# Expert tiles of 128 tokens regrouped as 16 pairs and 7 singles, with weights fetched per slot

## The chip, the core and the metric

The kernel runs on one core of a Trainium2 chip. TensorE (PE) multiplies, VectorE (DVE) and ScalarE (ACT) work element by element and read what PE wrote to PSUM, GpSimd (POOL) here does some elementwise work and issues the indexed transfers (gathers and scatters), and SyncE (SP) issues plain transfers. Each engine takes its instructions in the order of the program and waits on semaphores. The metric is the device time of one execution in microseconds.

## The reference

The input is 8 sequences of 256 tokens with 128 features. After a layer norm, two branches are added to it: a retention layer of 16 heads, and a mixture of 8 experts of which every token takes two:

```
scores = einsum('bnd,ed->bne', xn, expert_tokens)
_, topk_idx = top_k(scores, 2)
for i in range(8):
    w = mean(topk_idx == i, axis=-1)            # 0 or 0.5
    h = gelu(xn @ W1[i] + b1[i])                # 128 -> 512
    h = gelu(h @ W2[i] + b2[i])                 # 512 -> 512
    outputs += (h @ W3[i] + b3[i]) * w          # 512 -> 128
```

Everything is float32. The biases are not zero.

## The kernel before, in words

First comes the retention stage: eight batches `b` of 256 tokens in a hand-written order on each engine. During batches 0 to 5, DVE also works out the routing in small chained instructions (`step`, counted by the semaphore `v_disp`; the constants `D_...` say after which count a result is there): for each of 4096 token-expert assignments a slot in a list, sorted by expert and padded to tiles of 128. The lists `gidx` and `sidx` hold for every tile the tokens to gather and to scatter to. `expert_of_tile` writes the expert of each tile to `exi`. Normed tokens lie in device memory as `xnd`.

The expert stage is a loop over 39 tiles of 128 tokens. For a tile, POOL gathers the rows (`gather`, into one of four `xg`), PE transposes them (`trans_x`), ACT copies them to `xf`, PE does the first layer, DVE adds the bias, ACT applies Gelu (`gelu1`), ACT and DVE split the result into a high and a low part (`h1h`, `h1l`). The second layer is 12 float32r matmuls with 512 moving columns: the hidden state is stationary and the weights move, high and low parts of both. DVE adds the bias, ACT applies Gelu, PE transposes four blocks (`trans2`), ACT copies, PE does the third layer, DVE scales and adds the bias (`out3`, into one of two `ys`), and POOL adds the rows to the output in device memory (`scatter`).

All weights of all eight experts lie in SBUF. Those of the second layer are loaded in 32 pieces of 128 x 512 and split into `w2h` and `w2l` beside the retention stage, the last twelve after it (`w2_high`, `w2_low`, `w2_both`). The matmuls pick the expert by a register. First-layer weights are copied to `w1c` by DVE for each tile (`fetch`).

PE's order per tile is second layer of t, input transpose of t+3, third layer of t-1, first layer of t+2, `trans2` of t. POOL's order is gather of t+4, then scatter of t-1; each scatter waits until the one before has landed, since both add to the same rows.

Of the kernel before, what the change touches and what calls it, by code (L numbers as in the profile page):

```python
# [15 lines left out]
NT = 39  # L16
NTP = 40
LATE = 3
# [9 lines left out]
C_REP = 1661  # L28
C_N = 2173
# [5 lines left out]
def constants():  # L35
# [17 lines left out]
    c[:, C_IT:C_IT + NTP] = np.arange(NTP)  # L53
    c[:, C_K:C_K + 16] = 128 * np.arange(16)
# [15 lines left out]
def moe_retention_kernel(nc, x, wqkv, wvo, gb, etokT, w1, w2, w3, b1t, b23, cf, cb, out):  # L70
# [4 lines left out]
    R0 = 16512  # L75
    W2H, W2L = R0, R0 + 65536
    W1O, W3O = R0 + 131072, R0 + 147456
    B2O, B3O = R0 + 163840, R0 + 180224
    F0 = R0 + 184320
    w2h = at("w2h", 8 * 2048, F32R, W2H)  # L80
    w2l = at("w2l", 8 * 2048, F32R, W2L)
    w1s = at("w1s", 8 * 512, F32, W1O)
    w3s = at("w3s", 8 * 512, F32, W3O)
    b2s = at("b2s", 8 * 512, F32, B2O)
    b3s = at("b3s", 8 * 128, F32, B3O)
    o = F0
    ident = at("ident", 128, F32, o); o += 512
    gidx = at("gidx", NTP, U32, o); o += 160
    sidx = at("sidx", NTP, U32, o); o += 160
    ex = at("ex", NTP, F32, o); o += 160  # L90
    exi = at("exi", NTP, I32, o); o += 160
    b1s = at("b1s", 32, F32, o); o += 128
    stg = [at(f"stg{i}", 512, F32, o + 2048 * i) for i in range(4)]; o += 8192
    G0 = o


    xg = [at(f"xg{i}", 128, F32, o + p) for i, p in enumerate((1536, 512, 1024, 0))]; o += 2048
    xf = [at(f"xf{i}", 128, F32, o + 512 * i) for i in range(2)]; o += 1024
    w1c = at("w1c", 512, F32, o); o += 2048
    g1 = at("g1", 512, F32, o); o += 2048  # L100
    h1h = at("h1h", 512, F32R, o); o += 2048
    h1l = at("h1l", 512, F32R, o); o += 2048
    g2 = at("g2", 512, F32, o); o += 2048
    h2t = [at(f"h2t{i}", 512, F32, o + 2048 * i) for i in range(2)]; o += 4096
    ys = [at(f"ys{i}", 128, F32, o + 512 * i) for i in range(2)]; o += 1024
    assert o <= 229368


    o = G0
    cs = at("cs", 384, F32, o); o += 1536  # L110
    small = at("small", C_REP - C_P, F32, o); o += 512
    cbs = at("cbs", B_N, BF16, o); o += 896
    wq = at("wq", 512, F32, o); o += 2048
    et = at("et", 8, F32, o); o += 32
    mv = at("mv", 32, F32, o); o += 128
    st = at("st", 96, F32, o); o += 384
    vs = at("vs", 128, F32, o); o += 512
    qr = [at("qr0", 256, F32, o), at("qr1", 256, F32, o + 1024)]; o += 2048
    kr = [at("kr0", 256, F32, o), at("kr1", 256, F32, o + 1024)]; o += 2048
    qh = at("qh", 256, F32R, o); o += 1024  # L120
    rstd = at("rstd", 16, F32, o); o += 64
    o += 32
    wv = at("wv", 256, F32, o); o += 1024
    gbt = at("gbt", 2, F32, o); o += 32
    xr = [at(f"xr{i}", 256, F32, o + 1024 * i) for i in range(2)]; o += 2048
    rt = at("rt", 256, F32, o); o += 1024
    sq = at("sq", 256, F32, o); o += 1024
    rn = at("rn", 256, F32, o); o += 1024
    ob = at("ob", 256, F32, o); o += 1024
    vr = at("vr", 32, F32, o); o += 128  # L130
    eps = at("eps", 1, F32, o); o += 32
    nb = at("nb", 16, F32, o); o += 64
    assert o <= 229368, o
    A0 = W2H + 40960
    B0 = W2L + 40960
    C0, D0, E0 = W3O + 10240, B2O, W1O + 10240

    o = A0
    oh = [at(f"oh{i}", 128, BF16, o + 256 * i) for i in range(8)]; o += 2048
    bt = at("bt", 16 * NTP, BF16, o); o += 1280  # L140

    s1 = at("s1", 128, F32, A0)
    cm = at("cm", 128, F32, A0 + 512)
    past = at("past", 7 * NTP, F32, A0)
    sc = at("sc", 128, F32, A0 + 1024)
    s0 = at("s0", 128, F32, A0 + 1536)
# [97 lines left out]
    def sync():  # L244
# [17 lines left out]
        for i in range(4):  # L262
            load_w2(i)
# [1058 lines left out]
```

## Time and profile before

| | |
|---|---|
| median of 3 runs | 378.18 us (377.08 to 378.86) |
| profiled execution, own time | 378.94 us |
| its span, first to last instruction | 377.2 us |
| mean granted TensorE clock | 0.953 |
| PE busy | 315.3 us, 84% |
| DVE, ACT, POOL busy | 238.7, 183.3, 181.3 us |
| HBM read, written | 21.61 MB, 4.65 MB |

The retention stage takes the first 150 us or so, then 14 us pass until the second layer of the first tile starts at 164.22, and the tiles run until the end. Busy time of PE counts overlapping matmuls once; a matmul's own duration holds its depth, so that the step from one start to the next says more.

### The profile page before, as it was taken

How to read it: one execution, taken by the hardware profiler on the slowest of the kernel's cores; microseconds unless marked ns; L12 is line 12 of the kernel's file. 1: busy time of each engine (PE TensorE's matmuls, PEld its weight loads, DVE VectorE, ACT ScalarE, POOL GpSimd, SP SyncE). 2: the span in 40 equal slices, each digit the busy share in tenths (PEclk: the TensorE clock that was granted, in tenths of full speed). 3: DMA queues.
4: the chain of work that ended last, by engine and by line, in shares of the span. 5: the costliest groups of instructions: out<-in, count | busy, mean ns of one | idle time of the engine just before them, and what ended most of it. 6: DMA issues, size and time to landing. Idle time of an engine off the chain costs nothing.

```text
span 377.2 us, 7594 instructions
## 1 busy us (share of the span) xinstructions
PE 315.3 (84%) x2304; PEld 269.6 (71%) x2304; DVE 238.7 (63%) x471; ACT 183.3 (49%) x390; POOL 181.3 (48%) x169
## 2 busy tenths in 40 slices
PE   0995958777686897459999999999999999999960
PEld 0793846656484675348888988898888889888850
DVE  5659899899989887744555454455545455555410
ACT  4463355466554675624554454455455445445420
POOL 8106256465655443752444455544455554444331
PEclk9999699899988999869999999999999999999995
DMA  8270292122231238801112221111221111222000
GB/s 260 93 223 30 76 323 78 56 58 56 57 106 40 89 108 330 295 22 16 22 28 28 29 30 19 29 24 24 30 28 27 23 21 27 30 24 24 5 2 0
DMA packets 25109, 26.31 MB, mean 70 GB/s; under 512 B 3712, under 2 KB 18048, under 8 KB 24944
## 3 DMA queue, kind: packets, MB, share of 16 engines
q1 hardware_dynamic: 14080, 13.69, 11.8%
q0 software_dynamic: 6864, 4.67, 9.1%
q10 hardware_dynamic: 4128, 7.47, 5.7%
q8 instruction: 22, 0.36, 0.4%
q14 instruction: 15, 0.12, 0.1%
HBM read 21.61 MB, written 4.65 MB: 70 GB/s over the span
## 4 chain that ended last, share of the span: by engine, by line
PE 68%; DVE 15%; issue 8%; ACT 3%; DMA 2%; POOL 1%; ACTq 0%; DVEq 0%; SPq 0%; POOLq 0%
PE ps L194 60%; PE ps L1186 5%; DVE qx L696 3%; DVE pt L703 2%; DVE tmp L672 2%; DVE w2l L737 1%; DMA xn<-in_x 1%; PE ps L1147 1%; PE ps L988 1%; DVE bt L613 1%; PE ps L994 1%; DVE kr L677 1%; DVE vr L716 1%; DVE bt L610 1%; DMA out<-ys,sidx 1%
## 5 line engine op out<-in xcount | busy, mean ns | idle before, releaser
L919 POOL DMA_INDIRECT out<-ys,sidx x39 | 62.0, 1589 | 95.0 <-DVE ys L775 90.4
L767 DVE TENSOR_TENSOR g<-ps,b2s 128x512 f32<-128x512 f32 x39 | 27.0, 691 | 79.9 <-PE ps L194 79.9
L194 PE MATMUL ps<-w2l,h1h 128*128 x156 | 65.4, 419 | 4.6 <-DVE w2l L737 4.6
L194 PE MATMUL ps<-w2h,h1h 128*128 x156 | 61.7, 396 | 0.0
L194 PE MATMUL ps<-w2h,h1l 128*128 x156 | 61.3, 393 | 0.0
L403 ACT CAST h1h<-g 128x512 fp32r<-128x512 f32 x39 | 24.1, 619 | 56.0 <-PE ps L194 55.9
L912 POOL DMA_INDIRECT xg<-xnd,gidx x39 | 39.1, 1004 | 15.7 <-issue 10.6
L397 ACT ACTIVATE g<-g 128x512 f32<-128x512 f32 x39 | 24.7, 634 | 42.6 <-DVE g L751 42.6
L888 POOL TENSOR_SCALAR_AFFINE_SELECT pt<-pt 128x512 f32<-128x512 f32 x24 | 16.3, 677 | 57.5 <-ACT pt L294 57.5
L194 PE MATMUL ps<-xf,w1c 128*128 128x128 f32 x312 | 41.4, 276 | 2.6 <-ACT xf L393 2.0
L194 PE MATMUL ps<-w3s,h2t 128*128 x312 | 41.2, 275 | 0.8 <-ACT h2t L413 0.8
L194 PEld LDWEIGHTS ps<-w3s,h2t 128*128 128x128 f32 x312 | 38.0, 191 | 4.4 <-issue 1.0
L194 PEld LDWEIGHTS ps<-xf,w1c 128*128 128x128 f32 x312 | 38.0, 192 | 3.2 <-issue 3.1
L194 PEld LDWEIGHTS ps<-w2l,h1h 128*128 128x128 f32 x156 | 29.8, 191 | 9.8 <-issue 4.9
L751 DVE TENSOR_TENSOR g<-ps,b1s 128x512 f32<-128x512 f32 x39 | 27.0, 691 | 15.1 <-PE ps L194 14.4
L194 PEld LDWEIGHTS ps<-w2h,h1h 128*128 128x128 f32 x156 | 29.6, 190 | 7.0
L194 PE MATMUL ps<-qx,kst 128*128 128x512 f32 x64 | 31.8, 501 | 2.9 <-DVE pt L703 1.5
L194 PEld LDWEIGHTS ps<-w2h,h1l 128*128 128x128 f32 x156 | 29.9, 192 | 5.1
L407 ACT ACTIVATE g<-g 128x512 f32<-128x512 f32 x39 | 24.6, 630 | 8.0 <-DVE g L767 3.2
L761 DVE TENSOR_TENSOR h1l<-g,h1h 128x512 fp32r<-128x512 f32 x39 | 28.0, 719 | 0.6 <-ACT h1h L403 0.6
L703 DVE TENSOR_TENSOR pt<-ps,cs 128x512 f32<-128x512 f32 x40 | 27.0, 680 | 1.3 <-PE ps L194 1.1
L696 DVE CAST qx<-ps 32x512 fp32r<-32x512 f32 x32 | 22.2, 693 | 6.2 <-PE ps L194 5.7
(137 smaller groups left out, 599.6 us busy)
## 6 DMA issues: line engine op xcount, KB each, us to landing
stg<-in_w SPq DMA_DIRECT2D x24, 256.0 KB, 2.7
b2s<-in_b ACTq DMA_DIRECT2D x1, 2048.0 KB, 10.4
w2l<-in_w SPq DMA_DIRECT2D x4, 512.0 KB, 5.9
w1s<-in_w ACTq DMA_DIRECT2D x1, 1280.0 KB, 7.5
xn<-in_x SPq DMA_DIRECT2D x4, 256.0 KB, 4.7
xnd<-xn SPq DMA_DIRECT2D x1, 1024.0 KB, 6.1
xr<-in_x SPq DMA_DIRECT2D x8, 128.0 KB, 3.4
out<-ob SPq DMA_DIRECT2D x8, 128.0 KB, 3.2
```

The source lines that it names most:

```text
L194: mm = lambda o_, l, r, s=True, p=True: T.matmul(o_, l, r, start=s, stop=p, skip_group_check=True)
L397: A.activation(g1[:], g1[:], ACT.Gelu).then_inc(a_g1, 1)
L403: A.copy(h1h[:], g1[:]).then_inc(a_h1h, 1)
L407: A.activation(g2[:], g2[:], ACT.Gelu).then_inc(a_g2, 1)
L696: e = V.tensor_copy(qv[rows, :, i, m, :], r3(ps[(0, 5)[i]][rows, :], 2, 256))
L703: V.tensor_tensor(r3(pt[n % 6][:], 4, 128), r3(ps[3 + n % 2][:], 4, 128), cmask.unsqueeze(1).to_broadcast([128, 4, 128]), ALU.mult).then_i ...
L751: V.tensor_tensor(r3(g1[:], 4, 128), r3(ps[0][:], 4, 128), b1s[:, bass.ds(vregs[t] * 4, 4)].unsqueeze(2).to_broadcast([128, 4, 128]), ALU. ...
L761: V.tensor_tensor(h1l[:], g1[:], h1h[:], ALU.subtract).then_inc(v_h1l, 1)
L767: V.tensor_tensor(g2[:], ps[2][:], b2s[:, bass.ds(vregs[t] * 512, 512)], ALU.add).then_inc(v_b2, 1)
L912: G.indirect_dma_start(xg[t % 4][:], None, xnd, bass.IndirectOffsetOnAxis(ap=gidx[:, t:t + 1], axis=0)).then_inc(d_g[t % 4], 16)
L919: G.indirect_dma_start(out, bass.IndirectOffsetOnAxis(ap=sidx[:, t:t + 1], axis=0), ys[t % 2][:], None, bounds_check=NTOK - 1, oob_is_err= ...
L1186: e = T.transpose(ps[3][:, 128 * c:128 * c + 128], g2[:, 128 * c:128 * c + 128], ident[:])
```

## The change

The 39 tiles become 23 slots: 16 pairs of two tiles of the same expert and then 7 single tiles (`SLOTS`). The routing gives each expert its full pairs in the first 32 tile numbers and its odd tile in the last seven, with 18 more chained instructions.

For a pair, the moving operand is 256 tokens wide. In the second layer the weights are now stationary and the hidden state moves, so that the result comes out transposed already: 48 matmuls of 256 columns for two tiles, no `trans2`, and bias and Gelu in one ACT instruction per 256 columns, read from PSUM. Singles keep the form of before, but their bias comes after the transposes.

Weights are fetched per slot by SP: `wa` (first- and third-layer weights and biases, 128 x 1160, four buffers) and `raw` (second layer, 128 x 2048, three buffers). ACT casts the whole 128 x 2048 to `w2h`, DVE subtracts to `w2l` in place; for the first three slots POOL does the latter, beside the retention stage. There are four `ys` instead of two, and the scatter stands three tiles behind the loop's tile.

```
+NPAIR, NONE = 16, 7
+SLOTS = [(2 * i, 2 * i + 1) for i in range(NPAIR)] + [(2 * NPAIR + j,) for j in range(NONE)]
...
-    D_GT, D_MSK, D_POS, D_IDX, D_EXP, D_ALL = 5, 7, 13, 24, 27, 33
+    D_MSK, D_POS, D_EXP, D_ALL = 7, 23, 45, 51
...
+        def load_weights(i, which):
+            t = last(i)
+            e = nc.sync.value_load(exi[0:1, t:t + 1], min_val=0, max_val=NEXP - 1)
+            if which != "w2":
+                if i >= 4:
+                    P.wait_ge(v_ys, last(i - 4) + 1)
+                P.dma_start(was[i % 4][:], wa[bass.ds(e, 1)]...).then_inc(d_wa[i % 4], 16)
+            if which != "wa":
+                if i >= 3:
+                    P.wait_ge(t_l2, last(i - 3) + 1)
+                P.dma_start(raw[i % 3][:], w2[bass.ds(e, 1)]...).then_inc(d_w2[i % 3], 16)
...
+        for i in range(PRE, NS):          # SP, after the retention stage; PRE = 3
+            load_weights(i, "w2")
+            if i + 1 < NS:
+                load_weights(i + 1, "wa")
...
+        for i in range(NS):               # ACT
+            if i + 1 < NS:
+                for t in SLOTS[i + 1]:
+                    gelu1(t)
+                    h1_high(t)
+            if i and wid(i - 1) == 128:
+                gelu2(last(i - 1))
+            if i + 2 < NS:
+                copy_xf(i + 2)
+                if i + 2 >= PRE:
+                    w2_high(i + 2)
+            if wid(i) == 256:
+                for t in SLOTS[i]:
+                    gelu2(t)
...
+        for i in range(NS):               # DVE
+            if i >= 2:
+                for t in SLOTS[i - 2]:
+                    out3(t)
+            if i and wid(i - 1) == 128:
+                copy_g2(last(i - 1))
+            if i + 1 < NS:
+                for t in SLOTS[i + 1]:
+                    h1_low(t)
+            if PRE <= i + 2 < NS:
+                w2_low(i + 2)
...
+        for t in range(NT):               # POOL
             if t + 4 < NT:
                 gather(t + 4)
+            if t == 3:
+                G.wait_ge(d_ob, 16 * NB)
+            if t == first(slot_of[t]):
+                half_b3(slot_of[t])
+            if t >= 3:
+                scatter(t - 3)
...
+            if wid(i) == 256:             # layer2, PE
+                for k in range(2):
+                    out_ = bank[:, 256 * k:256 * k + 256]
+                    for c in range(4):
+                        ...
+                        mm(out_, wl[:, w], hi[:, cc], c == 0, False)
+                        mm(out_, wh[:, w], lo[:, cc], False, False)
+                        e = mm(out_, wh[:, w], hi[:, cc], False, c == 3)
...
+        for i in range(NS):               # PE
+            if i + 1 < NS:
+                for t in SLOTS[i + 1]:
+                    layer1(t)
+            if i and wid(i - 1) == 128:
+                trans2(last(i - 1))
+            if i + 2 < NS:
+                for t in SLOTS[i + 2]:
+                    trans_x(t)
+            for t in SLOTS[i]:
+                layer2(t)
+            if i:
+                for t in SLOTS[i - 1]:
+                    layer3(t)
```

One turn of the loops over slots is called turn i below.

POOL's order in the expert stage, before: a gather (L912) and a scatter (L919) in turn. The first row gathers tile 6, the second scatters tile 1, the third gathers tile 7; `d_g`, `t_gT`, `d_s` and `v_ys` are the semaphores of gathers landed, input transposes done, scatters landed and `ys` written.

```order
L912 DMA xg2_67<-xnd,gidx_56 128x128 [waits t_gT]
L919 DMA out_0<-ys1_79,sidx_57 2048x128 [waits d_s,v_ys]
L912 DMA xg3_68<-xnd,gidx_56 128x128 [waits t_gT]
L919 DMA out_0<-ys0_78,sidx_57 2048x128 [waits d_s,v_ys]
L912 DMA xg0_65<-xnd,gidx_56 128x128 [waits t_gT]
```

The same place now, with tiles 0, 8, 1, 9 and 2 in the DMA rows (L903 scatters, L896 gathers, L883 halves a slot's third-layer bias):

```order
L903 DMA out_0<-ys0_76,sidx_82 2048x128 [waits v_ys,d_ob]
L896 DMA xg0_62<-xnd,gidx_81 128x128 [waits t_gT]
L883 TENSOR_SCALAR wa2_60<-wa2_60 128x128 [waits d_wa2]
L903 DMA out_0<-ys1_77,sidx_82 2048x128 [waits d_s,v_ys]
L896 DMA xg1_63<-xnd,gidx_81 128x128 [waits t_gT]
L903 DMA out_0<-ys2_78,sidx_82 2048x128 [waits d_s,v_ys]
```

The gather of tile t+4 stood behind the scatter of tile t-2, six tiles back, and stands now behind that of tile t-4, eight tiles back.

PE's order around one tile before, from the end of one second layer to the start of the next (L1147 is the input transpose, L1186 `trans2`, L194 a matmul):

```order
L194 MATMUL ps2<-w2h_49,h1h_73 128x512
L1147 MATMUL ps5<-ident_55,xg1_66 128x128 [waits a_xf,d_g1]
L194 ISA [waits v_ys,a_h2]
L194 MATMUL ps4<-w3s_52,h2t1_77 128x128
...
L194 MATMUL ps0<-xf0_69,w1c_71 128x128 [waits v_w1c,v_b1,a_xf]
L194 MATMUL ps0<-xf0_69,w1c_71 128x128 x3
L1186 MATMUL ps3<-ident_55,g2_75 128x128 [waits a_h2,a_g2]
L1186 MATMUL ps3<-ident_55,g2_75 128x128 x3
L194 ISA [waits v_b2,v_h1l]
L194 MATMUL ps2<-w2l_50,h1h_73 128x512
```

PE now, from the end of one pair's third layer (L150 is a matmul, L1129 the input transpose):

```order
L150 MATMUL ps5<-wa3_61,h21_74 128x128 x3
L150 MATMUL ps2<-xf0_66,wa2_60 128x256 [waits a_g1,d_wa2,a_xf]
L150 MATMUL ps2<-xf0_66,wa2_60 128x256
L150 MATMUL ps0<-xf0_66,wa2_60 128x256 [waits a_h2,d_wa2,a_xf]
L150 MATMUL ps0<-xf0_66,wa2_60 128x256
L1129 MATMUL ps5<-ident_80,xg2_64 128x128 [waits v_ys,a_xf,d_g2]
L1129 MATMUL ps5<-ident_80,xg3_65 128x128 [waits v_ys,a_xf,d_g3]
L150 MATMUL ps1<-h1h1_70,w2l0_52 128x256 [waits a_h2,v_w2l,v_h1l]
```

The input transposes moved from behind a second layer to the place between the first and the second layer.

SP in the expert stage now (before, it had nothing to do there); `exi` is the list of experts, L225 loads `wa`, L229 loads `w2`:

```order
L225 ISA [waits v_ys]
L225 DMA wa2_60<-in_wa 128x1160
L221 TENSOR_LOAD exi_84
L221 ISA x2
L229 ISA [waits t_l2]
L229 DMA raw0_55<-in_w2 128x2048
```

Every load of second-layer weights is queued behind a load of `wa` that waits for `ys`.

## Rows read from the trace of the kernel before

**Rows 1.** The page: busy us, share of the span, instructions of each engine.
```profile
PE 315.3 (84%) x2304; PEld 269.6 (71%) x2304; DVE 238.7 (63%) x471; ACT 183.3 (49%) x390; POOL 181.3 (48%) x169
```

**Rows 2.** Windows: stretch, length, busy PE, PEld, DVE, ACT, POOL (instructions), clock, DMA share, GB/s.
```profile
200.00:300.00 100.00, 100.00 (x650) 89.17 (x649) 52.59 (x100) 49.47 (x99) 50.58 (x39) 1.00 0.18 26
```

**Rows 3.** The chain that ended last: start us, us, what; two of its repeating pieces.
```profile
252.51 2.76 PE ps L194 x12
255.38 1.79 PE ps L194 x16
```

**Rows 4.** Timeline of one tile's period: start us, us, engine, line, operation.
```profile
254.53 0.99 POOL L912 DMA_INDIRECT xg<-xnd,gidx  x1 [0.31 <-issue]
...
256.62 0.28 DVE L775 SCALAR_TENSOR_TENSOR ys<-ps,b3s 128x128 f32<-128x128 f32 x1
...
257.73 1.59 POOL L919 DMA_INDIRECT out<-ys,sidx  x1 [2.21 <-DVE ys L775]
...
259.62 1.00 POOL L912 DMA_INDIRECT xg<-xnd,gidx  x1 [0.30 <-issue]
```

**Rows 5.** Timeline of PE in the retention stage: matmuls with 256 moving columns.
```profile
129.67 1.03 PE L194 MATMUL ps<-xnt,wq 128*128 128x256 f32 x4
...
134.51 0.28 PE L194 MATMUL ps<-kl,repm 128*128 128x256 f32 x1
...
135.22 0.28 PE L194 MATMUL ps<-kl,repm 128*128 128x256 f32 x1
```

**Rows 6.** Timeline of PE at the start of the expert stage.
```profile
159.17 0.47 PE L1147 MATMUL ps<-ident,xg 128*128 128x128 f32 x1
164.22 0.79 PE L194 MATMUL ps<-w2l,h1h 128*128 x1 [4.58 <-DVE w2l L737]
...
168.55 0.27 PE L1147 MATMUL ps<-ident,xg 128*128 128x128 f32 x1
```

**Rows 7.** DMA issues, us to landing: from 200 to 300 us, and last from 150 to 161 us.
```profile
out<-ys,sidx POOLq DMA_INDIRECT x20, 3.2
xg<-xnd,gidx POOLq DMA_INDIRECT x19, 2.5
...
xg<-xnd,gidx POOLq DMA_INDIRECT x2, 6.6
```

**Rows 8.** DMA issues of the whole span: KB each, us to landing.
```profile
b2s<-in_b ACTq DMA_DIRECT2D x1, 2048.0 KB, 10.4
...
w1s<-in_w ACTq DMA_DIRECT2D x1, 1280.0 KB, 7.5
```

**Rows 9.** Groups by form: busy us, mean ns, idle before; elementwise instructions of several widths.
```profile
L767 DVE TENSOR_TENSOR g<-ps,b2s 128x512 f32<-128x512 f32 x39 | 27.0, 691 | 79.9 <-PE ps L194 79.9
...
L379 ACT CAST w2h<-stg 128x512 fp32r<-128x512 f32 x24 | 14.0, 618 | 0.0
...
L737 DVE TENSOR_TENSOR w2l<-stg,w2h 128x512 fp32r<-128x512 f32 x4 | 4.5, 1126 | 0.0
...
L732 DVE TENSOR_TENSOR ob<-ps,xr 128x256 f32<-128x256 f32 x8 | 3.4, 420 | 0.2
...
L300 ACT CAST kh<-kr 128x256 fp32r<-128x256 f32 x8 | 3.2, 405 | 5.3 <-DVE kr L677 5.3
...
L555 DVE TENSOR_TENSOR cm<-ne,small 128x128 f32<-128x128 f32 x1 | 0.3, 292 | 0.0
```

**Rows 10.** Timeline at the end: the last tiles' third layer, `out3` and scatters.
```profile
361.60 0.39 PE L194 MATMUL ps<-w2h,h1h 128*128 x1
...
361.82 1.05 PE L194 MATMUL ps<-w3s,h2t 128*128 x8
...
363.02 0.29 DVE L775 SCALAR_TENSOR_TENSOR ys<-ps,b3s 128x128 f32<-128x128 f32 x1 [0.22 <-PE ps L194]
...
364.09 1.55 POOL L919 DMA_INDIRECT out<-ys,sidx  x1 [3.09 <-DVE ys L775]
...
367.64 1.55 POOL L919 DMA_INDIRECT out<-ys,sidx  x1 [1.99 <-DMA out<-ys,sidx]
```

More of the change, by code:

```diff
@@ L389, in copy_xf @@
[L389 to L397 removed]
+            A.wait_ge(d_w2[i % 3], 16 * (i // 3 + 1))
+            if i >= 3:
+                A.wait_ge(t_l2, last(i - 3) + 1)
+            A.copy(w2h[i % 3][:], raw[i % 3][:]).then_inc(a_w2h, 1)
@@ new lines, in copy_xf @@
+        def copy_xf(i):
+            n = wid(i)
+            A.wait_ge(t_gT, last(i) + 1)
+            if i >= 2:
+                A.wait_ge(t_l1, last(i - 2) + 1)
+            A.copy(xf[i % 2][:, 0:n], ps[5][:, 0:n]).then_inc(a_xf, 1)
+        def gelu1(t):
+            i = slot_of[t]
+            n = wid(i)
+            bank = ps[big["l1", t] % 3]
+            A.wait_ge(t_l1, t + 1)
+            if i:
+                A.wait_ge(v_h1l, last(i - 1) + 1)
+            A.wait_ge(d_wa[i % 4], 16 * (i // 4 + 1))
+            half = t - first(i)
+            for k in range(512 // n):
+                c = 512 // n * half + k
+                e = A.activation(g1[:, n * c:n * c + n], bank[:, n * k:n * k + n], ACT.Gelu,
+                                 bias=was[i % 4][:, W_B1 + c:W_B1 + c + 1])
+            e.then_inc(a_g1, 1)
@@ L415, in scalar @@
+            half = t - first(i)
+            for k in range(512 // n):
+                c = 512 // n * half + k
+                e = A.activation(h2[i % 2][:, n * c:n * c + n], bank[:, n * k:n * k + n], ACT.Gelu,
+                                 bias=was[i % 4][:, W_B2 + c:W_B2 + c + 1])
+            e.then_inc(a_h2, 1)
         A.dma_start(small[:], cf[:, C_P:C_REP]).then_inc(d_rep, 16)
@@ L837, in vector @@
             evac(8 * b + 6)
-            if not more:
-                bias1(0)
             if b == 0:
@@ L1152, in layer1 @@
-        def layer1(t):
-            T.wait_ge(a_xf, t + 1)
-            if t:
-                T.wait_ge(v_b1, t)
-            T.wait_ge(v_w1c, t + 1)
-            if t < 2:
-                expert(t)
-            for c in range(4):
-                e = mm(ps[0][:, 128 * c:128 * c + 128], w1c[:, 128 * c:128 * c + 128], xf[t % 2][:])
+            if i:
+                T.wait_ge(a_xf, i)
+            if i >= 4:
+                T.wait_ge(v_ys, last(i - 4) + 1)
+            half = 128 * (t - first(i))
@@ new lines, in trans_x @@
+            T.transpose(ps[5][:, half:half + 128], xg[t % 4][:], ident[:]).then_inc(t_gT, 1)
+        def layer1(t):
+            i = slot_of[t]
+            n = wid(i)
+            T.wait_ge(a_xf, i + 1)
+            T.wait_ge(d_wa[i % 4], 16 * (i // 4 + 1))
+            bank = free_bank(("l1", t))
+            for k in range(512 // n):
+                c = 512 // n * (t - first(i)) + k
+                e = mm(bank[:, n * k:n * k + n], was[i % 4][:, W_1 + 128 * c:W_1 + 128 * c + 128], xf[i % 2][:, 0:n])
```

631 lines of the change are left out of this document (271 added, 360 removed).

## The prediction

> **What bounds the kernel now.** I read the busy table first, then the chain of waits, then one period of the expert stage in the timeline, and last the DMA landings. TensorE (PE) is busy 84% of the span, and between 200 and 300 us it has no idle time at all, at a granted clock of 1.00, its 2.4 GHz level [rows 1, 2]. The chain stays on PE, repeating 2.76 us (12 matmuls of the second layer) and 1.79 us (16 instructions) every 5.09 us [rows 3]: 39 tiles at PE's own pace. The reader should see that no other engine matters there. In rows 4 GpSimd (POOL) waits 2.21 us for `ys`, scatters, and issues a gather 0.30 us behind the scatter's end. That gather was for a tile three turns ahead, so the scatter in front of it cost nothing. This slack is what the change spends.
>
> **PE's work per pair.** Everything in this stage runs back to back, so the spacing counts and not the duration.
> - Second layer: 24 matmuls of 512 columns at 2.76/12 = 0.230 us [rows 3] become 48 of 256 columns. The trace has float32r matmuls of that width with a new stationary operand each time: six steps from 134.51 to 135.22 are 0.118 us each [rows 5]. 48 x 0.118 = 5.68 against 5.52 us. That the weight load could set the pace instead is excluded by the same rows.
> - First layer: four x N=256 float32 matmuls are eight instructions. Four take 1.03 us with the depth of the last one in it [rows 5]; with 0.28 for that depth, as in the rows below it, the step is at most 0.25, and two of 128 columns are 0.224. I take 0.208: 1.66 us. Before, 16 at 0.112 (1.79/16) [rows 3] = 1.79.
> - The eight transposes of the second layer's output go: -0.9 us. Third layer (1.79) and two input transposes (0.22) stay.
>
> Sum for a pair: 5.68 + 1.66 + 1.79 + 0.22 = 9.35 us against 2 x 5.09 = 10.18. If PE set the pace, 16 pairs would give 13.3 us back. The vector engine (DVE) loses its bias adds and weight copies, ScalarE (ACT) gets more small Gelus. Per pair ACT then has eight instructions of 256 columns at 0.405, two casts at 0.618, a copy of 0.4 and the cast of a slot's weights, 1.9 (below): 6.8 us; DVE 0.6 + 1.4 + 2.3 = 4.3 [rows 9]. Both fit under 9.35 and so cost nothing by themselves.
>
> **The new wait on POOL.** In turn i of the main loop PE runs first layer of slot i+1, transposes of slot i+2, second layer of slot i, third layer of slot i-1. POOL's loop is still one gather, one scatter per tile, but the scatter is now of tile t-3 and the gather of tile t+4. So the gather of tile 2i+5, which PE transposes in turn i, stands behind the scatter of tile 2i-3, and that tile's third layer is the last thing of turn i-1 (POOL's order, in the part on the change). From the end E of that third layer, by rows:
> - `out3` starts at +0.15 and ends at +0.44 (362.87 to 363.02, 0.29 long) [rows 10].
> - scatter of tile 2i-4 starts 0.83 us after its `ys` (256.90 to 257.73) [rows 4]: +1.27. It holds POOL 1.59: +2.86.
> - gather of tile 2i+4: +3.16 to +4.16.
> - scatter of tile 2i-3 waits until the other has landed: 3.2 us from issue [rows 7], +4.47, and starts 0.84 later, as 364.09 + 2.71 to 367.64 did [rows 10], 3.55 us from scatter to scatter: +5.3, to +6.9.
> - gather of tile 2i+5: +7.2, lands 2.5 us later [rows 7]: +9.7.
>
> PE has only the first layer, 1.66 us, to do meanwhile, then stands about 8 us before the second layer, which is queued behind the transposes. What follows is 0.1 + 0.22 + 5.68 + 1.79 + 0.16 (depth) = 7.95, and the loop closes: 17.65 us a pair at least, as against 10.18.
>
> Two costs come on top. First, traffic: at that moment SyncE (SP) starts loading 580 KB and 1024 KB (SP's order, same part). With the DMA engines full, gathers took 6.6 us to land instead of 2.5 [rows 7]. Bounds per loop: 0 (the weights slip between) and 4.1 + about 2 on the scatter = 6. The weights are through after some 7 us and the critical gather starts after that, so I take 1.0, near the quiet row. Second, the clock: PE was idle 4.58 us, and resumed at 164.22 at half clock (1.2 GHz); 12 matmuls took until 168.55, 4.33 us for 2.76 [rows 6]. That is +1.6. Bounds: 0 if the clock held, 7.5 if second and third layer (7.47 us) ran at the half level throughout. That row is the only restart after an idle time of this kind, so I stay near it, a little above since the gap is longer: 2.0, and 0.15 for the transposes. Pair loop: 17.65 + 1.0 + 2.15 = **20.8 us**.
>
> On the clock the Trainium skill, "TensorE: Matmul & The Clock Gate", section "HAM oscillation — how this bites in real kernels", describes a kernel whose matmul bursts are parted by DMA waits and which starts every burst cold. By that rule every one of these turns pays; with a clock that held, the pair loop would be 18.65 and the whole 26 us shorter. The trace agrees for its gap of 4.58 us. On traffic the Trainium skill, "DMA: Bandwidth & Descriptors", section "Queues, rings and completion order", says each DMA engine takes packets from its queue rows in turn, so that a gather is slowed by weights but not held until they are through. By it the 1.0 us is nearer than 6; the 6.6 us landing agrees with slowed.
>
> **The weights' own loop.** `wa` of slot j waits for `ys` of slot j-4, which `out3` writes at the start of turn j-2, and `w2` of slot j is queued behind it on SP; then ACT casts 2048 columns, DVE subtracts 2048 columns, and the next `out3` is queued behind that subtract. Loads of 1280 and 2048 KB landed after 7.5 and 10.4 us, with others beside them [rows 8]; for 1604 KB with little beside it I take 7.5 (bounds 6.5 and 9.5). Cast: 0.405 at 256 columns and 0.618 at 512 give 1.90; subtract: 0.420 and 0.691 give 2.32 (4.5 at the 1.126 of one form) [rows 9]. 7.5 + 1.9 + 2.3 + 0.3 (`out3`) + five handovers of about 0.1 = **12.5 us** a turn. It stays under 20.8 for pairs and is hidden there by PE's wait for the gather; if that wait is gone, it is what comes next (rival 1). For singles the gather is not late (eight tiles back is an old slot), so this loop sets 12.5 where the tile took 5.09.
>
> **Attention.** 18 more chained DVE instructions on counts (13 to 23, 27 to 45 in the `D_` constants), at most 0.29 each [rows 9]: up to 5.2; DVE is on the chain there, while ACT and POOL lose weight splits. I take +4 (bounds 1 and 6). The 4.58 us wait for the split weights before 164.22 goes [rows 6]; late next is the copy of slot 1's inputs behind the first Gelus, about where PE was at 159.2.
>
> **Sum against the profiled span of 377.2.** Turn 0 starts at 159.2 + 4 = 163. It has a cold first layer, 3.4, transposes 0.4, second layer about 6.2: 173. Turn 1, undisturbed: 9.35, to 182. Turns 2 to 13 have the full stall: 12 x 20.8 = 250, to 432. Turn 14 waits only for one gather (issued at +3.2, landing 4 us, then 7.95 and 2.15): 17, to 449, `ys` at 449.7. Then six turns of the weights' loop, 75: 524.7. Left are one second layer at half clock 5.1, copies and transposes 5.5, another second layer 2.8, and the 15.6 us that stood before after the last second layer began to drain (361.60 to 377.2): 29. Span 553.7. The profiled run took 1.7 us more than its span (378.94), 0.8 above the median of 378.18: **554 us**, slower by 46%.
>
> **Rivals.**
> 1. *Only the weights' loop binds.* If the gathers are somehow early, pairs run at 12.8 (two `out3`). From 182: 13 turns are 166, six more 75, tail 29.7, total 453, so 454 us. For it: the loop is there in the code in any case. Against: POOL's order.
> 2. *PE keeps the pace* (the other side). Gathers and weights stay hidden, and 9.35 holds: 377.2 - 13.3, with the saved start and the longer routing even: about 365 us, faster. It decides if the second gather lands within 1.7 us of E and the weights' loop under 9.35. Rows give 9.7 and 12.5, so little speaks for it but an ordering that I misread.
> 3. *Loaded landings.* Weights and gathers collide fully, each loop near 26: 12 x 5 more, 615 us. For it: 6.6 against 2.5. Against: the critical gather starts late in the load.
>
> **Chances.** Forecast 82%, with its own range 515 to 595 (pair loop 18.5 to 23.5, weights' loop 11.5 to 14.5, routing 1 to 6). Rival 1: 8%; rival 2: 4%; rival 3: 6%. The range 500 to 600 leaves out the rivals. A difference under 0.5% can't be told from none. Faster 0.04, same 0.01, slower 0.95.
>
> **What would show it.** PE idle before the transposes of nearly every pair, released by the gather's DMA, some 8 us; POOL's second scatter of a pair released by the first one's landing; granted clock below 1 through the pair stage, second layer at 0.118 and 0.213 us spacing; a pair period near 20.8 and a single period near 12.5 with DVE's subtract followed at once by `out3`. It would be wrong if PE's idle time ended on ACT or DVE, or if the pair period were under 15.

## The result

Measured on one chip beside the kernel before: **605.3 us** (603.5 to 606.5, 4 runs) against 378.5 us, a ratio of 1.600 with a 95% interval of 1.593 to 1.606. Forecast was 554 us: the direction and the mechanism hold, the size does not, and the time lies above the range's end of 600 us. The profiled span grew from 377.2 to 603.9 us.

### The profile page after: what moved, and what is told of

It is laid out like the page before. It is cut to its first block, busy times and chain, and to the rows that moved or that the text cites. A ratio compares the mean times of both kernels' runs of the same rounds, so it can differ in the third digit from the quotient of the medians.

```text
span 603.9 us, 7127 instructions
## 1 busy us (share of the span) xinstructions
PE 344.5 (57%) x2432; PEld 301.9 (50%) x2432; DVE 210.6 (35%) x390; ACT 210.3 (35%) x433; POOL 185.0 (31%) x178
## 3 DMA queue, kind: packets, MB, share of 16 engines
q1 hardware_dynamic: 15872, 42.54, 20.8%
## 4 chain that ended last, share of the span: by engine, by line
PE 35%; DMA 34%; DVE 11%; issue 10%; POOL 4%; ACT 3%; SPq 1%; DVEq 0%; POOLq 0%; ACTq 0%
PE ps L150 32%; DMA out<-ys,sidx 23%; DMA xg<-xnd,gidx 7%; POOL out L903 4%; DMA raw<-in_w 4%; DVE qx L706 2%; DVE pt L713 1%; DVE ys L770 1%; PE ps L1129 1%; ACT w2h L355 1%; DVE tmp L682 1%; DMA xn<-in_x 1%; PE ps L960 1%; PE ps L966 1%; DVE kr L687 1%
## 5 line engine op out<-in xcount | busy, mean ns | idle before, releaser
L903 POOL DMA_INDIRECT out<-ys,sidx x39 | 63.9, 1640 | 312.5 <-DVE ys L770 220.9
L755 DVE TENSOR_TENSOR w2l<-raw,w2h 128x2048 fp32r<-128x2048 f32 x20 | 45.9, 2293 | 227.3 <-ACT w2h L355 227.3
L1129 PE MATMUL ps<-ident,xg 128*128 128x128 f32 x39 | 16.1, 425 | 170.3 <-DMA xg<-xnd,gidx 166.1
L1129 PEld LDWEIGHTS ps<-ident,xg 128*128 128x128 f32 x39 | 6.9, 177 | 179.8 <-DMA xg<-xnd,gidx 175.1
L150 PE MATMUL ps<-h1h,w2l 128*128 128x256 f32 x256 | 85.7, 335 | 0.0
L150 PE MATMUL ps<-h1l,w2h 128*128 128x256 f32 x256 | 83.1, 325 | 0.0
L150 PE MATMUL ps<-h1h,w2h 128*128 128x256 f32 x256 | 82.6, 323 | 0.0
L150 PEld LDWEIGHTS ps<-h1h,w2l 128*128 128x128 f32 x256 | 61.1, 239 | 0.0
L150 PEld LDWEIGHTS ps<-h1l,w2h 128*128 128x128 f32 x256 | 60.4, 236 | 0.0
L150 PEld LDWEIGHTS ps<-h1h,w2h 128*128 128x128 f32 x256 | 59.9, 234 | 0.0
L355 ACT CAST w2h<-raw 128x2048 fp32r<-128x2048 f32 x23 | 43.7, 1901 | 37.9 <-DMA raw<-in_w 37.9
L896 POOL DMA_INDIRECT xg<-xnd,gidx x39 | 41.9, 1074 | 11.2 <-issue 10.9
L150 PE MATMUL ps<-wa,h 128*128 128x128 f32 x312 | 39.7, 280 | 1.2 <-ACT h L401 1.2
L150 PEld LDWEIGHTS ps<-wa,h 128*128 128x128 f32 x312 | 38.4, 196 | 2.2 <-ACT h L401 1.5
L150 PE MATMUL ps<-xf,wa 128*128 128x256 f32 (+1 forms) x184 | 38.8, 355 | 0.0
L150 PE MATMUL ps<-qx,kst 128*128 128x512 f32 x64 | 30.9, 487 | 3.6 <-DVE pt L713 1.6
```

Source lines behind the costliest of these rows:

```text
L150: mm = lambda o_, l, r, s=True, p=True: T.matmul(o_, l, r, start=s, stop=p, skip_group_check=True)
L355: A.copy(w2h[i % 3][:], raw[i % 3][:]).then_inc(a_w2h, 1)
L755: V.tensor_tensor(w[:], raw[i % 3][:], w2h[i % 3][:].bitcast(F32), ALU.subtract).then_inc(v_w2l, 1)
L896: G.indirect_dma_start(xg[t % 4][:], None, xnd, bass.IndirectOffsetOnAxis(ap=gidx[:, t:t + 1], axis=0)).then_inc(d_g[t % 4], 16)
L903: G.indirect_dma_start(out, bass.IndirectOffsetOnAxis(ap=sidx[:, t:t + 1], axis=0), ys[t % 4][:], None, bounds_check=NTOK - 1, oob_is_err= ...
L1129: T.transpose(ps[5][:, half:half + 128], xg[t % 4][:], ident[:]).then_inc(t_gT, 1)
```

## The profile after

The page, engines' busy time, against [rows 1]: PE is busy 29 us more in a span 227 us longer.

```profile
PE 344.5 (57%) x2432; PEld 301.9 (50%) x2432; DVE 210.6 (35%) x390; ACT 210.3 (35%) x433; POOL 185.0 (31%) x178
```

The same stretch as [rows 2]: PE busy 48.5 of 100 us, clock 0.71 where it was 1.00.

```profile
200.00:300.00 100.00, 48.53 (x303) 45.14 (x302) 16.66 (x20) 26.66 (x48) 24.21 (x20) 0.71 0.26 77
```

The chain that ended last, one turn of it (start, us, what). It answers to [rows 3], where only PE stood.

```profile
303.51 8.35 DMA out<-ys,sidx
...
312.74 1.61 POOL out L903
314.35 0.30 issue
314.66 2.52 DMA xg<-xnd,gidx
...
317.23 0.47 PE ps L1129
317.70 8.97 PE ps L150 x64
...
326.90 0.29 DVE ys L770
327.19 0.62 issue
327.81 8.18 DMA out<-ys,sidx
```

The same turn in the timeline (start, us, engine, line, operation; in brackets the idle time before it and what ended it). It answers to [rows 4].

```profile
302.40 0.49 DVE L770 SCALAR_TENSOR_TENSOR ys<-ps,wa 128x128 f32<-128x128 f32 x2 [4.77 <-PE ps L150]
303.06 0.33 SPq L225 DMA_DIRECT2D wa<-in_wa  x1
...
303.51 1.60 POOL L903 DMA_INDIRECT out<-ys,sidx  x1 [12.50 <-DVE ys L770]
...
304.15 0.33 SPq L229 DMA_DIRECT2D raw<-in_w  x1
...
305.42 1.00 POOL L896 DMA_INDIRECT xg<-xnd,gidx  x1 [0.31 <-issue]
...
312.06 0.48 PE L1129 MATMUL ps<-ident,xg 128*128 128x128 f32 x1 [7.97 <-DMA xg<-xnd,gidx]
312.74 1.61 POOL L903 DMA_INDIRECT out<-ys,sidx  x1 [5.48 <-DMA out<-ys,sidx]
314.66 1.03 POOL L896 DMA_INDIRECT xg<-xnd,gidx  x1 [0.30 <-issue]
...
317.23 0.47 PE L1129 MATMUL ps<-ident,xg 128*128 128x128 f32 x1 [4.69 <-DMA xg<-xnd,gidx]
```

Read it as a loop: `ys`, scatter a, its landing, scatter b, gather, its landing, PE's burst, `ys`. Every link is one that the prediction named, in its order. Two loads of weights are issued around scatter a (303.06 and 304.15); the first lands 3.7 us after its issue, the second 7.6 us after its own, at 311.7. Scatter a lands at 311.86.

Scatter a of pair 0 starts at 177.85, that of pair 12 at 477.09: **24.94 us a turn**, forecast 20.8. The last seven tiles show the weights' own loop. Each subtract waits for the cast, the cast for `raw`, and `ys` stands right behind the subtract:

```profile
521.77 2.29 DVE L755 TENSOR_TENSOR w2l<-raw,w2h 128x2048 fp32r<-128x2048 f32 x1 [10.95 <-ACT w2h L355]
523.98 0.48 DVE L770 SCALAR_TENSOR_TENSOR ys<-ps,wa 128x128 f32<-128x128 f32 x2
...
534.78 2.29 DVE L755 TENSOR_TENSOR w2l<-raw,w2h 128x2048 fp32r<-128x2048 f32 x1 [9.12 <-ACT w2h L355]
536.99 0.28 DVE L770 SCALAR_TENSOR_TENSOR ys<-ps,wa 128x128 f32<-128x128 f32 x1
```

Up to 537 us the landing of the scatter that frees the next `ys` comes within 0.1 us of the subtract's end, so that there two paths are equally long; behind it the weights' loop stands alone, at 12.3 to 13.6 us a tile.

## Where the 50 us beyond the forecast are

| piece | forecast | measured | difference |
|---|---|---|---|
| end of turn 1 | 182 | 176.6 | -5.4 |
| turns 2 to 13 | 12 x 20.8 | 12 x 24.94 | +49.6 |
| turn 14 | 17 | 20.3 | +3.3 |
| six single turns | 75 | 79.3 | +4.3 |
| tail | 29 | 27.9 | -1.1 |

The differences add up to 50.7 us (the forecast's own total, 553.7, has 12 x 20.8 rounded up to 250). So one number needed explaining: the landing of scatter a, 8.4 us in the turn shown, where 3.2 plus 1.0 was forecast. The packets of single microseconds (count, MB, share of the 16 engines' time) show how it comes about. First 307 to 308 us, 4 us after the scatter's issue began and 2 us after it ended; then the next one:

```profile
q1 hardware_dynamic: 37, 0.30, 108.3%
```

```profile
q1 hardware_dynamic: 36, 0.22, 53.6%
q0 software_dynamic: 74, 0.04, 34.1%
```

q1 is SP's queue with the weights, q0 that of POOL. From 303 to 308 no packet of q0 is in the records; the first comes 4.8 us after the scatter's start, and they then come as q1 thins out. In the kernel before, where little else moves, a scatter's first packet is recorded 2.2 us after its start. So 2.6 us of the delay lie ahead of the first packet and the rest behind it. I took as theory that the amount of weights that SP put out at that moment holds scatter a, and as first rival that an indexed scatter of the new form is slow by itself.

## The experiments

All change the changed kernel. e1 to e4, e5 to e8, e9 and e10, and e11 and e12 each ran on one chip beside the kernel before, which took 376.2, 376.9, 377.8 and 376.8 us there. The changed kernel was timed only beside the 378.5 us above; the chips differ by 0.6% at most by the kernel before, which is small against what follows. One run each, except e9 (4), e11 and e12 (6). In the experiments below, scatter a and scatter b are the first and second scatter of a pair, and gather a and gather b stand behind them.

**e1, both weight loads light.** The edit, shortened:

```
-  P.dma_start(was[i % 4][:], wa[e])
+  P.dma_start(was[i % 4][:, k0:W_N], wa[e][:, k0:W_N])   # k0 = 1032 from slot 4 on
-  P.dma_start(raw[i % 3][:], w2[e])
+  P.dma_start(raw[i % 3][:, 0:k1], w2[e][:, 0:k1])       # k1 = 128 from slot 3 on; cast, subtract too
```

> From slot 4 on only the bias part of wa (64 KB of 580) and from slot 3 on only 128 of 2048 columns of w2 (64 KB of 1024) are fetched, and only these are cast and subtracted; the rest of the buffers keeps an older slot's weights, so the expert outputs are those of other weights. Theory T (the weights that SP loads in the same moment hold up the landing of a pair's first scatter; 8.5 us instead of 3.2): the scatter lands in about 3.3 us, a pair's turn falls from 24.9 to about 19.7 us, singles lose the load and most of cast and subtract and go to 6 or 7 us; total near 500 us. Rival S (an accumulating scatter that starts right after a gather or another scatter is slow by itself): landing stays near 8.5, pair turn near 24.9, total near 565, all of the gain in the singles.

Measured 498.1 us, the theory's number. Landings from 180 to 420 us (count, KB, median us):

```profile
wa<-in_wa SPq DMA_DIRECT2D x12, 64.0 KB, 1.8
raw<-in_w SPq DMA_DIRECT2D x12, 64.0 KB, 1.9
xg<-xnd,gidx POOLq DMA_INDIRECT x24, 2.5
out<-ys,sidx POOLq DMA_INDIRECT x24, 3.3
```

These are the quiet values of [rows 7]. A turn takes 20.1 us, at a clock of 0.75. The rival is out.

**e2, six gather buffers.** `xg` and its semaphores `d_g` go from 4 to 6, with `gather(t + 6)` ahead of `scatter(t - 3)`.

> Six gather buffers instead of four, so that the gather that PE needs in turn i is issued before the scatters of the pair just finished. If the gather queued behind the scatter is what the turn waits for, PE's wait before the transposes goes. Next is the chain of scatters (each waits for the one before to land) or the weights' own loop (12.8). T: first scatter 8.5, second 3.2, plus 0.8 each: 13.4 us a turn, total near 460 us. S: both 8.5: 18.7 us a turn, total near 525. If POOL's order were not the cause: total stays at 600.

Measured 459.7 us; a pair turn takes 13.7 us, close to T. So it was the gather queued behind the scatter that the turn waited for, although scatter a lands hardly faster (8.0 us in the mean). Up to 284 us gather b, which now takes 4.5 to 5 us to land, is still on the chain in every other turn. Behind that, two loops end within 0.2 us of each other, and e2 does not tell them apart: scatter a, its landing, scatter b, its landing (which frees a `ys`), `ys`; and the weights' own loop of load, cast, subtract and `ys`:

```profile
293.53 1.62 POOL L903 DMA_INDIRECT out<-ys,sidx  x1 [5.83 <-DMA out<-ys,sidx]
294.40 2.29 DVE L755 TENSOR_TENSOR w2l<-raw,w2h 128x2048 fp32r<-128x2048 f32 x1 [7.10 <-ACT w2h L355]
295.46 2.12 POOL L896 DMA_INDIRECT xg<-xnd,gidx  x1 [0.30 <-issue]
...
296.61 0.48 DVE L770 SCALAR_TENSOR_TENSOR ys<-ps,wa 128x128 f32<-128x128 f32 x2
```

Scatter b lands 3.1 us after its start, at 296.63, and the subtract ends at 296.69.

**e3, weights fetched only after the slot's input transposes.**

```
                 P.wait_ge(v_ys, last(i - 4) + 1)
+                P.wait_ge(t_gT, last(i) + 1)
```

> All weights are fetched as before, but the load of a slot's wa (and w2 behind it) also waits until PE has transposed that slot's inputs, so that weights move while PE does the second layer and not while the pair's scatters and gathers move. T: the first scatter lands in about 3.3 us; but the weights come later, and DVE's subtract now stands in front of the next out3: turn about 22 us instead of 24.9; singles 2.5 us longer each; total near 585. S: scatter still 8.5, turn about 27, total near 640.

Measured 593.8 us, turn 23.2 us (T: 585 and 22). All the weights still move, and scatter b starts 4.2 us behind scatter a (changed kernel: 9.4), so amount alone is not the cause, but amount at that moment. Little is won, since the landing of `raw`, now behind the transposes, stands on the path itself, with the cast and the subtract behind it:

```profile
310.84 1.90 ACT L356 CAST w2h<-raw 128x2048 fp32r<-128x2048 f32 x1 [8.95 <-DMA raw<-in_w]
```

**e4, the second scatter of a pair does not wait for the first.** The two tiles of a pair belong to one expert and hold different tokens, so their rows differ.

```
-            if t:
-                G.wait_ge(d_s, 16 * t)
+            if t and t == first(slot_of[t]):
+                G.wait_ge(d_s0, 16 * ((t + 1) // 2))
+                if t > 1:
+                    G.wait_ge(d_s1, 16 * (t // 2))
...
```

Tiles with an even number count on `d_s0` and the others on `d_s1`; `out3` waits on the one of its buffer.

> The second scatter of a pair no longer waits for the first to land (same expert, so no token twice; each parity has its own semaphore, and a slot's first scatter waits for all before). The second gather is issued some 5 us earlier, but if weights hold up everything on the indexed queue (T), it lands no earlier than they are through, about 10 us after the first scatter's issue instead of 13.7: turn about 21 us, total near 555. S: the two scatters and gathers cost their own 3 us more each, turn 18 to 19, total near 530.

Measured 546.3 us, between the two; the turn of 20.4 us is near T's. Scatter b starts 3.9 us behind a, gather b is issued at 304.74, and still PE's first transpose starts only at 307.12, after 7.64 us:

```profile
302.82 1.62 POOL L905 DMA_INDIRECT out<-ys,sidx  x1 [0.18 <-issue]
304.74 1.03 POOL L896 DMA_INDIRECT xg<-xnd,gidx  x1 [0.30 <-issue]
307.11 0.18 PEld L1132 LDWEIGHTS ps<-ident,xg 128*128 128x128 f32 x1 [8.04 <-DMA xg<-xnd,gidx]
307.12 0.94 PE L1132 MATMUL ps<-ident,xg 128*128 128x128 f32 x2 [7.64 <-DMA xg<-xnd,gidx]
```

The weights there were issued at 298.44 and 299.54, the second landing 7.2 us later, at 306.7. Gather a, issued at 300.80, lands 6.3 us later, 0.3 us behind them: gathers are held like scatters. Not waiting for scatter a to land was worth 4.5 us a turn.

**e5 and e6, one load light at a time.** The edits of e1, on w2 alone and on `wa` alone.

> From the fourth slot on only 128 of the 2048 columns of w2 are fetched, cast and subtracted (that part of the computation is left out); w1, the biases, w3 and b3 (wa, 580 KB) are fetched in full. Theory: the pair's first scatter lands when the packets that the SP queue put out before it are through, so what holds it is their amount. With 580 KB in place of 1604 KB it lands in 4 to 5 us (8.5 in the changed kernel, 3.3 with both loads light), a pair turn takes 20.5 to 21.5 us, the whole about 510 us. Rival: what holds it is that any large load starts there, whatever its size: landing near 8 us, turn 24 to 25, the whole about 555 us.

> The other half: from the fifth slot on only the last 128 of the 1160 columns of wa are fetched (w1, the biases and w3 of the slot are left out of the computation), w2 in full (1024 KB). Theory (amount in front of the scatter): landing 6 to 7.5 us, a pair turn 22.5 to 24 us, the whole about 580 us. Rival (any large load): the same 8 to 8.5 us as the changed kernel, turn 25, the whole 600 us. Second rival (the load issued ahead of the scatter, wa, is what counts, and w2, issued 0.6 us behind it, does not): landing near 3.5 us, turn 20, the whole about 545 us.

Measured 508.0 and 561.3 us. POOL's scatters, e5 and then e6:

```profile
301.20 1.60 POOL L905 DMA_INDIRECT out<-ys,sidx  x1 [12.71 <-DVE ys L772]
306.48 1.62 POOL L905 DMA_INDIRECT out<-ys,sidx  x1 [1.54 <-DMA out<-ys,sidx]
```

```profile
317.14 1.60 POOL L905 DMA_INDIRECT out<-ys,sidx  x1 [12.90 <-DVE ys L772]
324.06 1.62 POOL L905 DMA_INDIRECT out<-ys,sidx  x1 [3.18 <-DMA out<-ys,sidx]
```

Taking 0.88 us from landing to the next start, as at 311.86 and 312.74, the landing is 4.4 and 6.0 us in the turns shown; the medians of the twelve pair turns are 3.9 and 6.0. Turns are 20.5 and 22.2 us. Both rivals fail, the one where size does not matter and the one where only the load ahead of the scatter counts: w2 in full is issued 0.66 us behind the scatter and still delays it by 2.7 us over the quiet 3.3. e6's total came out 19 us under its expectation: some 12 us are pair turns just under the short end of what was expected, and the single tiles' loop shrank too (`raw` lands in 4.9 us without `wa` beside it).

**e7, PE kept busy in its waits.**

```
                 for t in SLOTS[i + 2]:
+                    if 1 <= i < 14:
+                        T.wait_ge(v_base, NB)
+                        for k in range(30 if t == first(i + 2) else 18):
+                            mm(ps[7][:, 0:448], cbs[:, 0:128], cbs[:])
                     trans_x(t)
```

> The changed kernel with extra bf16 matmuls of 448 columns on PE (result unused) in the two waits of a pair turn: 30 ahead of the pair's first transpose, 18 ahead of its second, 0.187 us each at the full clock, so 5.6 and 3.4 us of waits that last 8.0 and 4.7 us. Theory: of the turn's 9.3 us of expert matmuls 1.9 us are there only because PE waits ahead of them and its clock falls; kept busy it is granted more than 0.95, the burst takes 7.5 us, a turn 23.1 in place of 24.9, the whole about 582 us. Rival: the burst is long for another reason (its operands, its order): clock up, turn still 24.9, the whole 604 us or more.

Measured 595.5 us. From 290 to 390 us the granted clock is 0.97 (0.70 in the changed kernel), with PE now busy 85.6 of 100 us. The changed kernel first, then e7:

```profile
290.00:390.00 100.00, 46.42 (x297) 43.03 (x297) 16.66 (x20) 26.65 (x48) 25.24 (x21) 0.70 0.28 78
```

```profile
290.00:390.00 100.00, 85.56 (x531) 60.74 (x532) 16.93 (x21) 28.90 (x50) 26.87 (x22) 0.97 0.28 78
```

Over the same eight turns a turn falls from 24.79 to 23.22 us, so the clock costs **1.6 us a turn** (forecast 2.15, expected here 1.8). The rival, a burst that is long for another reason, is out. The whole gains less than expected, since pair 2's scatter starts at 232.88 in place of 228.46: the extra matmuls also stand where there was no wait yet.

**e8, six buffers and both loads light.**

> Six gather buffers in place of four and both weight loads light from the fourth or fifth slot on (only 128 columns of w2 and 128 of wa are fetched; the rest of those weights is left out of the computation). Theory: with the loop over the gathers and scatters and the loop over the weights both gone the pairs run at PE's own pace, 9.35 us for 64 matmuls of 256 columns, 8 transposes and layer 3, at a clock near 1: pair turn 9.4 to 10.5 us, singles 5 to 7 us, the whole 365 to 380 us, so the paired tiles by themselves gain about 10 us of PE time on the kernel before and no more. Rival: two scatters per turn one behind the other, 3.3 us and 1.6 us of issue each, bound it next: pair turn 10.5 to 12 us, the whole 380 to 400 us.

Measured 365.3 us, 11.6 us under the kernel before. Twelve pair turns in a row take 9.3 to 9.4 us:

```profile
200.00:300.00 100.00, 100.00 (x791) 97.46 (x790) 23.35 (x53) 53.25 (x129) 63.99 (x54) 1.00 0.26 42
```

That is the measured value of pairing with the weights nearly free, 9.43 against 10.18 us for two tiles before, and the term of 9.35 in the prediction. The rival, two scatters in turn, is out: they fit into 9.4 us.

**e9 and e10, the loops loosened, and the weights' part of that alone.** e9 is e2 and e4 with this, e10 is this on the changed kernel; w2 goes ahead of `wa` on SP (and its wait, for a second layer, ends before `ys` does), its cast and subtract one turn later:

```
-        for i in range(PRE, NS):
-            load_weights(i, "w2")
-            if i + 1 < NS:
-                load_weights(i + 1, "wa")
+        load_weights(PRE, "w2")
+        for i in range(PRE + 1, NS):
+            load_weights(i, "both")            # and in it, w2 first
...
-                w2_high(i + 2)                 # ACT; DVE: w2_low(i + 2)
+                w2_high(i + 1)                 #           w2_low(i + 1)
```

> Only the last of these edits on the changed kernel: w2 fetched ahead of wa, cast and subtract one turn later. Theory: in the pairs the loop over gathers and scatters (24.9 us) is longer than that over the weights (13.2 us), so their turn stays at 24 to 26 us; the singles fall from 13.2 us to 9 to 11 us, the whole about 582 us. Rival (weights also bound the pairs): pair turn under 22 us, the whole under 560 us.

Measured 514.8 us; a pair turn is 20.4 us. My theory expected 24 to 26, and the rival, "weights bound the pairs", got the number by luck, without its reason: the gathers still close the loop. I had thought of when the weights are needed, not of when their packets leave:

```profile
316.14 0.33 SPq L225 DMA_DIRECT2D raw<-in_w  x1
...
317.79 0.49 DVE L769 SCALAR_TENSOR_TENSOR ys<-ps,wa 128x128 f32<-128x128 f32 x2 [4.95 <-PE ps L150]
318.45 0.33 SPq L230 DMA_DIRECT2D wa<-in_wa  x1
...
318.91 1.60 POOL L902 DMA_INDIRECT out<-ys,sidx  x1 [12.62 <-DVE ys L769]
...
323.73 1.62 POOL L902 DMA_INDIRECT out<-ys,sidx  x1 [1.08 <-DMA out<-ys,sidx]
```

The load of 1024 KB leaves 2.8 us ahead of scatter a in place of 0.6 us behind it. `wa` lands 3.9 us after its issue in this turn, so the weights are through 3.4 us after the scatter's start, and the scatter lands at 3.9. An edit that leaves every byte and every wait of POOL in place takes 90 us, 54 of them in the twelve pair turns (24.94 to 20.45). The edit changes the lead of w2 and the order of the two loads at once; which of them wins the time is not shown. Five kernels side by side, medians of the twelve pair turns, in us from scatter a's start:

| | first packet of POOL's queue | weights through | scatter a lands |
|---|---|---|---|
| changed kernel | 4.7 | 8.3 | 8.5 |
| e6, w2 only | 4.8 | 5.6 | 6.0 |
| e5, `wa` only | 2.5 | 3.5 | 3.9 |
| e10, w2 earlier | 2.7 | 3.6 | 4.0 |
| e1, both light | 2.2 | 2.6 | 3.4 |

(Weights through: landing of the later load, in the turns for which the trace has it, only two in e5. Scatter a lands: the time from scatter a to scatter b less 0.88 us. e1 has the quiet values.) Two things add up. Where w2 in full is issued 0.6 us behind the scatter, the scatter's first packet comes 2.5 us late, with `wa` full or light. And with any large load the scatter lands 0.2 to 0.5 us after the weights are through.

> A try at a version that keeps the whole computation and loosens all three loops: six gather buffers, the second scatter of a pair no longer waits for the first, and w2 of a slot is fetched ahead of wa and its cast and subtract come one turn later, so that out3 no longer stands behind them. Theory (the waits are the price, PE work per pair is 9.4 us): what is left as a loop are the pair's two scatters, 2 x 1.6 us of issue with a gather's 1.0 between and a landing of 5 to 8 us beside 1604 KB of weights, so a pair turn of 11 to 13 us, singles near 10 us, the whole 415 to 450 us: under the 459.7 us of six buffers alone, above the kernel before. Rival: the weights' landing of 7.7 us with cast and subtract still closes a loop of 13.5 us: 455 to 462 us. Second rival (everything hides, PE's pace 9.4 us): 375 to 385 us.

Measured 390.4 us (386.5 to 392.5), ratio 1.035 [1.028, 1.042]: under the theory's range and just above the second rival's. With w2 early the scatters' landing, which I had put at 5 to 8 us, was off the path of the pair turns: from 180 to 325 us POOL waits for no scatter, and PE waits 9.7 us, in six turns, for a gather. Pair turns alternate between 9.4 and 11 to 13, and single turns take 7.0 us.

**e11 and e12, a version to beat both.** e11 is e9 with eight gather buffers. e12 also casts a single's w2 ahead of the Gelu of the slot before:

```
+            if PRE <= i + 1 < NS and i and wid(i - 1) == 128:
+                w2_high(i + 1)
             if i and wid(i - 1) == 128:
                 gelu2(last(i - 1))
...
```

> The kernel of e9 with eight gather buffers in place of six, so that a gather is issued two pairs ahead of its transposes. In e9 a pair turn takes 10.6 us in the mean over 14 turns (alternately 9.4 and 11 to 13), PE waits for xg in every second one, 9.7 us in all, and its own work is 9.43. Theory (what is left in the pairs is that wait and the clock lost behind it): every turn 9.4 to 9.6 us, 14 x 1.2 = 15 us less, the whole 374 to 378 us, a tie with the kernel before. Rival: the wait is for the gather's landing beside 1604 KB of weights in the queues, whenever it is issued, and comes back as a wait for the scatters: 386 to 391 us as in e9.

> e11 with one more change, for the single tiles alone: ACT casts w2 of the next slot ahead of gelu2 of the slot before, not behind it. In e9 a single's turn is 7.0 us and goes round copy_g2 0.7, transposes 0.7, gelu2 1.1, copy_xf 0.3, cast 1.9, subtract 2.3; PE waits 1.6 us of it. Theory: with the cast ahead of gelu2 that loop opens, and the singles take 5.5 to 6.5 us: 4 to 8 us less than e11, 368 to 373 us, under the kernel before by 1 to 2 per cent. Rival: the landing of a single's 1604 KB (4.8 us, then 4.3 us, in part beside each other) is next behind the cast, near 6.5 to 7 us a turn: within 3 us of e11.

Measured **371.7 us** (369.8 to 374.2), ratio 0.988 [0.983, 0.992], and 370.5 us (369.9 to 376.4), ratio 0.984 [0.981, 0.988]. e11 came out a little better than its theory: a gain of 1.2%, small but outside the spread of the runs. Thirteen pair turns in a row take 9.3 to 9.4 us:

```profile
200.00:300.00 100.00, 100.00 (x792) 97.46 (x791) 44.76 (x54) 67.92 (x125) 75.43 (x53) 1.00 0.68 196
```

This has the same PE figures as e8, with 196 GB/s of transfers beside it in place of 42. e12 against e11: the intervals overlap, and nothing like 4 to 8 us is gained. A single's turn is 7.0 us in both, so the theory fails, and the total moved by less than the two differ from run to run. The rival's "within 3 us" holds, but that the landing is what follows was not shown. In e11's singles PE waits for the copy of the second layer's output, behind the subtract on DVE (from 300 us: total, times, longest):

```profile
PE ps L1176 <- DVE g L760: 11.5, 7, 2.5
```

## Why the prediction was right in kind and wrong in size

- **Bound before, PE's work per pair.** Right: 9.35 forecast, 9.43 in e8 and e11.
- **The new wait on POOL.** Right, link by link: `out3` to scatter 1.1 us, 1.6, landing of gather b 2.5, PE idle 7.97 us before the first and 4.69 before the second transpose (forecast about 8 in one piece; the 4.6 us more are the next term). e2 shows that it is the gather that makes PE wait. One reading was loose: before, the gather issued at 259.62 was not needed "three turns ahead", since PE transposed its tile at 265.30, one turn on. The slack behind its landing was some 3 us.
- **Traffic: the step that failed.** "First, traffic ... so I take 1.0, near the quiet row." Measured on the landing of scatter a: 8.4 less 3.2, **5.2 us** (8.5 and 5.3 in the median of twelve turns), and this one term carries the miss of 4.1 us a turn. The reasoning was that the critical gather starts when the weights are through. That was so (it lands in 2.5 us), but because the scatter ahead of it had waited for them. I weighed the load on the last link and not on the first, which is issued 0.6 us before the larger load. The upper bound, 6, was sound: with it the sum gives 25.8 a turn and 614 us, 9 us off; the middle of the bounds would have given 578. What I leaned on for the low end was the reading that a queue is slowed and not held. The Trainium skill, "DMA: Bandwidth & Descriptors", section "Queues, rings and completion order", says that an engine takes packets from its queue rows in turn. The trace agrees with that only from 308.3 us on, where packets of both queues are recorded beside each other; before, none of POOL's queue is recorded for 4.8 us after the scatter's start, 2.6 us longer than in the kernel before. Whether its packets wait in the engines or are late to be handed to them was not told apart.
- **Clock.** Mechanism right, 2.15 forecast, 1.6 by e7. In the turn shown the first fifteen or so matmuls of the second layer start 0.21 us apart and the others 0.12, the two spacings that the prediction named.
- **The weights' own loop.** Right: 12.5 forecast, 13.2 measured; the landing took 6.6 to 8.9 us where 7.5 was taken. It is hidden in pair turns, where the subtract ends 4 to 5 us before `ys`. That it is next behind the gather is not shown: e2's turn of 13.7 is near rival 1's 12.8 (453 us; e2 took 459.7), but there the chain of the two scatters, which the prediction did not have as a loop, ends within 0.2 us of it.
- **Attention.** Wrong in sign, small. The longer routing shows once (a batch's first `tmp` on DVE at 48.80, before 46.60) and is made good three batches on (93.13, before 95.17). Turn 0's first layer starts at 158.25, forecast 163.
- **Turn 14.** Its gather landed 6.8 us after issue, forecast 4: the same failed term again.
- **Rivals.** Rival 2's 365 us is what e8 measured once its condition held, with most of the weights left out; with all of them e11 took 371.7. Rival 3, which had a chance of 6%, came closest with 615. Its reason holds in part: scatter a collided with the weights, and so did gather a behind it (6.6 us to land), but gather b, the last link, did not.

The failed step and its price are shown by e1, e5, e6 and e10 together: traffic taken away, cut in two ways, and moved in time. Why a load issued behind the scatter keeps back the scatter's packets stays open.

## What to carry to other kernels

When a chain of small transfers is on the critical path, ask of every link, the first one above all, what large transfer is issued within a microsecond or two of it, and put the large one earlier: 2.8 us of lead, with w2 first, was worth 4.5 us a turn here. Count what a transfer on one engine's queue stands behind in turns of the loop, and give it one more buffer pair before shortening anything: two buffers gave 146 us, four with the other edits 234. A regrouping that saves 7% of PE's work can be read as worthless from its first timing; run it once with the new transfers made light, and see its own value (11.6 us, in a kernel that leaves most of the weights out) before judging it.

## What the runs showed of the hardware that I had not expected

- Beside a large load, an indexed scatter on POOL's queue landed 0.2 to 0.5 us after SP's plain loads were through (changed kernel, e5, e6, e10), also where the larger load was issued behind it. A gather did the same in e4, 0.3 us after them.
- A load of 1024 KB issued 0.6 us behind a scatter put the scatter's first packet at 4.7 to 4.8 us after its start (changed kernel, e6); without such a load it was at 2.2 (kernel before, e1), and with 580 KB issued 0.5 us ahead at 2.5 to 2.7 (e5, e10).
- 1604 KB needed 8.8 us from the first issue to the last landing with `wa` first and w2 1.1 us behind it, where w2 landed 5.0 us after `wa`, and 6.4 us with w2 first and `wa` 2.3 us behind (e10), where each landed about as fast as alone (4.8 and 4.0 us; alone 4.9 in e6 and 3.7 in e5). Why the order or the spacing should matter is open.
- Weights at 196 GB/s and 1.6 MB a turn cost PE nothing in the pair turns of e11: PE is busy 100 of 100 us at the full clock. In the singles a turn is 7.0 us in e11 and 5.4 in e8, where the loads, the cast and the subtract are all light; which of the three costs there was not told apart.
- POOL's own time for a gather was 1.0 us, and 2.0 to 2.5 where it ran beside DVE's subtract of 2.29 us (128 x 2048, two inputs from SBUF), as at 295.46 in e2. In e2, e9 and e11 all 40 gathers that overlap a subtract by more than 0.5 us took 1.96 us or more, and of those that overlap none, not one took over 1.3. In e8, which is e2 with light loads and a subtract of 128 columns, none of the pair turns' gathers took over 1.03 us. That the subtract and not the loads is the cause was not tested by itself, and the longer gather was hidden in these kernels.
